# Attention and expert layer on one core: in pairs 6 and 7 of the attention, the transpose of a normalized tile is issued behind a step's two transposes of probabilities instead of ahead of them

## The chip, the core and the metric

One NeuronCore of a Trainium2 chip runs the whole program. The metric is the device time of one execution in microseconds (us); the time of a kernel is the median of several executions.

## What is computed

The reference is a layer of two parts over x of shape 2 x 2048 x 1024 in float32. Cut to what matters here:

```python
def attention(x, wq, bq, wk, bk, wv, bv, wo, bo):      # 16 heads of 64
    q, k, v = (split_heads(x @ w.T + b) for w, b in ((wq, bq), (wk, bk), (wv, bv)))
    scores = einsum('bqhd,bkhd->bhqk', q, k) / 8, causal mask
    return merge_heads(softmax(scores) @ v) @ wo.T + bo
x = x + layernorm(attention(layernorm(x)))
x = x + layernorm(expert_ffn(layernorm(x)))            # 8 experts, gate by argmax
```

Only the attention part, and of it the way from `layernorm(x)` to q, k and v for the second of the two sequences, is touched.

## The kernel before

**Numbers in two halves.** All large products run on TensorE in float16, each operand as a high and a low half (`hi`, `lo`), with three products per tile: low x high, high x low, high x high.

**Pairs and steps.** There are 16 pairs of heads (`PAIRS`): pairs 0 to 7 belong to the first sequence, pairs 8 to 15 to the second. A pair is worked off in 17 steps (`NSTEP`). A step covers up to 8 blocks of 128 keys for each of the pair's two heads, so it is two tasks, and a pair has 34 tasks. In step i of pair p the engines do the following (the `body` function of each engine):

- TensorE (L608): `scores` of the step three ahead (`LAG = 3`), then a part of a projection (`project`, L573) of the next pair's q, k or v, then `times_v` (L535) of step i itself, which multiplies the transposed probabilities `pt` by v.
- VectorE: the row maxima of the scores, and the first read of a finished projection. ScalarE: exponentials (`probs`, L914) and their high half (`hl`, L921), the high halves of the projections and of the weights. GpSimd: the low half of the probabilities (L1072).
- SyncE (SP, L429): the DMAs. For the step three ahead it issues two transposes `pt<-hl` (`transpose_probs`, L412), one per head, each of 128 x 2048 float16 numbers. It also loads the next weights (`w_raw`, L410), stores finished rows (`o_scratch`, L426), and loads and stores the tiles of the second sequence.

The order of SyncE's issues is the order in which its `body` is written. There is no scheduler. Each engine works in its own order and waits for semaphores.

**Rings.** `hl` and `pt` each hold five tasks. `transpose_probs` waits until GpSimd has finished the low half of its task (`p_lo_done`) and until `times_v` has read the ring's old content, five tasks back (`pv_done`). ScalarE in turn waits, before it writes `hl` again, until the transpose of the task five back has landed (`pt_done`, L920).

**The normalized tiles of the second sequence.** Over pairs 0 to 6 the 16 tiles of 128 rows of the second sequence are normalized beside the attention and stored in `xn_scratch` (L439). In pairs 6 and 7 they are read back with a transpose, `arena<-xn_scratch` (`transpose_x`, L401), again 128 x 2048 float16 numbers each. This comes late because the destination `xt` (in `arena`) still holds the first sequence until the projections of pair 7 have read it:

```python
TURN_CHUNKS = [0, 1, 3, 2]
TURN_TILES = [4 * c + i for c in TURN_CHUNKS for i in range(4)]
TURN_STEPS = {"pre": {i: n for n, i in enumerate((6, 7, 9, 10, 11, 13, 14, 16))},
              "turn": {i: 8 + n for n, i in enumerate((0, 1, 3, 4, 5, 7, 8, 9))}}
```

"pre" is pair 6, "turn" is pair 7. Eight of the transposes stand in steps 6, 7, 9, 10, 11, 13, 14 and 16 of pair 6, eight in steps 0, 1, 3, 4, 5, 7, 8 and 9 of pair 7. Numbered 0 to 15 in that order, numbers 0 to 3 fill chunk 0 of `xt`, 4 to 7 chunk 1, 8 to 11 chunk 3, and 12 to 15 chunk 2.

**Who needs them.** During pair 7 TensorE projects for pair 8, the first of the second sequence. By `UNITS` and `UNIT_STEPS` its units come as k and v of chunk 0 in steps 0 and 1, k of chunk 1 in step 2, v of chunk 1 and q of chunks 0 and 1 in steps 3 to 6, k of chunk 3 in step 7, v and q of chunk 3 in steps 8 to 11, k of chunk 2 in step 12, then v and q of chunk 2. Before a unit of a chunk, `project` waits for that chunk's transposes (L580 to L583):

```python
if p == HALF_PAIRS:
    tiles = LN_TILES - PE_TILES + 4 * (TURN_CHUNKS.index(c) + 1)
    for i in range(4):
        pe.wait_ge(xt_done[i], 4 * tiles)
```

So number 7 is needed in step 2 of pair 7, number 11 in step 7, and number 15 in step 12. TensorE works in order: while it waits there, `times_v` of the same step waits behind it.

Of the kernel before, what the change touches and what calls it, by code (L numbers as in the profile page):

```python
# [41 lines left out]
HALF_PAIRS = PAIRS // B  # L42
# [110 lines left out]
LN_TILES = S // P  # L153
# [6 lines left out]
def norm_tiles(p, i, part):  # L160
    return [tile for tile, at in NORM_STEPS.items() if at[part] == (p, i)]
# [4 lines left out]
# [3 lines that stand above are left out]
# [20 lines left out]
def attend_phase(nc, x, w_pairs, mask_in, xn_scratch, o_scratch, arena, fin):  # L189
    with ExitStack() as ctx:  # L190
# [48 lines left out]
        xn_stored = sem("xn_stored")  # L239
# [19 lines left out]
        unit_done = sem("unit_done")  # L259
# [66 lines left out]
        def weight_at(p, m):  # L326

            return 3 * p + ({"k": 1, "v": 2, "q": 3} if p else {"v": 1, "k": 2, "q": 3})[m]

        def next_split(p, i):  # L330

            p, i = divmod(p * NSTEP + i, NSTEP)
            kind = KIND.get(p, "mid")
            m = SPLITS[kind].get(i) if p >= 0 else None
            target = p + 1 if m == "q" or kind == "first" and i == 1 else p + 2
            return (target, m) if m and target < PAIRS else None

        def units_before(p, needed):

            return N_UNIT * p + max(u for u, unit in enumerate(order_of(p)) if unit in needed) + 1  # L340
# [14 lines left out]
        def half_done(p):  # L355

            return first_step(p, N_ROUND // 2)
# [9 lines left out]
        def pt_of(n):  # L367
            return pt[:, 2 * PT_AT[n]:2 * (PT_AT[n] + TASK_BLOCKS[n]), :]
# [24 lines left out]
        @block.sync  # L393
        def _(sp):
            def load_x(tile, sem_, b, t):
                sp.dma_start(tile, x_view[b, t]).then_inc(sem_, 16)

            def transpose_x(n, i, source):

                tok = i * P  # L400
                sp.dma_start_transpose(xt.rearrange("p l k n -> p (l k) n")[:, :, tok:tok + P], source).then_inc(  # L401
                    xt_done[n % 4], 16)

            def load_first_weight(m):
                sp.dma_start(first_raw[m], w_pairs[0, WHICH[m]]).then_inc(first_loaded[m], 16)

            def load_weight(p, m):
                if weight_at(p, m) > 1:
                    sp.wait_ge(w_lo_done, weight_at(p, m) - 1)
                sp.dma_start(w_raw[:], w_pairs[p % HALF_PAIRS, WHICH[m]]).then_inc(w_loaded, 16)  # L410

            def transpose_probs(p, i):  # L412
                for h in range(2):
                    n = NTASK * p + 2 * i + h
                    read = max([n - T_RING] + PT_BEFORE[n]) + 1
                    if read >= 1:
                        sp.wait_ge(pv_done, read)
                    sp.wait_ge(p_lo_done, n + 1)
                    sp.dma_start_transpose(pt_of(n), hl_of(n, 2)).then_inc(pt_done[n % T_RING], 16)

            def store_rows(p, half):

                sp.wait_ge(o_lo_done, 2 * p + half + 1)
                for which in range(2):
                    first = min(slot_of(rounds_of(p)[r][which]) for r in range(4 * half, 4 * half + 4))
                    sp.dma_start(o_scratch[p // HALF_PAIRS, first:first + 4, :, p % HALF_PAIRS].rearrange("t p c -> p t c"),  # L426
                                 o_hl[:, which].rearrange("p t l c -> p t (l c)")).then_inc(o_stored, 16)

            def body(p, kind):  # L429
                for i in range(NSTEP):  # L430
                    n = TURN_STEPS.get(kind, {}).get(i)
                    if n is not None:
                        tile = TURN_TILES[n]
                        sp.wait_ge(xn_stored, 16 * (tile + 1))
                        sp.wait_ge(unit_done, units_before(HALF_PAIRS - 1, [(m, tile // 4) for m in "qkv"]))
                        transpose_x(LN_TILES + n, tile, xn_scratch[tile])
                    for tile in norm_tiles(*((p, i - 1) if i else (p - 1, NSTEP - 1)), 2):
                        sp.wait_ge(xn_lo_done, LN_TILES + tile + 1)
                        sp.dma_start(xn_scratch[tile], xn[:]).then_inc(xn_stored, 16)  # L439
                        if tile + 1 < LN_TILES:  # L440
                            load_x(x_in[:], x_loaded[X_RING], 1, tile + 1)
                    if p == 0 and i == 0:
                        load_x(x_in[:], x_loaded[X_RING], 1, 0)
                    step = step_of(p, i, kind)
                    if step:
                        transpose_probs(*step)
                    split = next_split(p, i - 1)
                    if split:
                        target, m = split
                        after = {"q": (target + 1, "k"), "k": (target, "v"), "v": (target, "q")}[m]  # L450
                        if after[0] < PAIRS:
                            load_weight(*after)

                    if kind == "last" and i == NSTEP - LAG:
                        fin["load_o"](sp, 0)
                        fin["load_x"](sp, 0)
                    if i == (half_done(p) + 2 if kind != "last" else NSTEP - LAG):
                        store_rows(p, 0)
                    if p > 0 and i == 2:
                        store_rows(p - 1, 1)  # L460

                    if kind == "last":
                        for k in ([0, 1] if i == 0 else [i + 1] if i < KT - 2 else []):
                            if k == 0:
                                sp.wait_ge(s_done, NTASK * (PAIRS - 1))
                            if k == 4:
                                sp.wait_ge(pv_done, NTASK * (PAIRS - 1))
                            if k == 6:
                                sp.wait_ge(w_lo_done, 3 * PAIRS)
                            sp.dma_start(wo_raw[k], fin["w_view"][k]).then_inc(wo_loaded[k], 16)  # L470
                    if kind == "last" and i == KT - 1:
                        sp.wait_ge(unit_done, N_UNIT * PAIRS)
                        sp.wait_ge(mix_set, 2)
                        for tile, source in fin["row_loads"]:
                            sp.dma_start(tile, source).then_inc(rows_loaded, 16)
                    if kind == "last" and i == KT:

                        sp.wait_ge(wo_lo_done, 1)
                        sp.dma_start(wo_raw[KT - 1], fin["w_view"][KT - 1]).then_inc(wo_loaded[KT - 1], 16)
                    if kind == "last" and KT <= i < KT + 3:  # L480
                        for tile, source in fin["loads"][2 * (i - KT):2 * (i - KT + 1)]:
                            sp.dma_start(tile, source).then_inc(fin_loaded, 16)
                    if kind == "last" and i == NSTEP - LAG:
                        fin["load_o"](sp, 1)
                        fin["load_x"](sp, 1)
                if kind == "last":
                    store_rows(p, 1)

            load_x(x_first[0], x_loaded[0], 0, 0)
            load_first_weight("v")  # L490
            sp.dma_start(fin["ident"][:], fin["ident_in"]).then_inc(consts_loaded, 16)
            sp.dma_start(mask[:], mask_in).then_inc(consts_loaded, 16)
            for i in range(1, X_RING):
                load_x(x_first[i], x_loaded[i], 0, i)
                if i in (3, 5):
                    load_first_weight({3: "k", 5: "q"}[i])
            for i in range(LN_TILES):
                sp.wait_ge(xn_lo_done, i + 1)
                if i + X_RING < LN_TILES:
                    load_x(x_first[i % X_RING], x_loaded[i % X_RING], 0, i + X_RING)  # L500
                if i >= PE_TILES:
                    transpose_x(i, i, first_hl(i))
            load_weight(1, "k")
            for i in range(LAG):
                if i == 2:
                    load_weight(1, "v")
                transpose_probs(0, i)
            pairs(body)
# [1319 lines left out]
```

## Time and profile before

| | us |
|---|---|
| median of 3 executions (2395.73 to 2400.45) | 2397.23 |
| the profiled execution | 2399.07 |
| its span, first to last instruction | 2396.9 |
| TensorE busy (95% of the span) | 2274.4 |
| ScalarE busy (73%) | 1746.3 |
| VectorE busy (71%) | 1690.6 |
| GpSimd busy (69%) | 1654.6 |

The profile comes from one execution. Busy times are sums over the span and mix stages with different limits. In it PE is TensorE's matmuls, PEld its weight loads, DVE VectorE, ACT ScalarE, POOL GpSimd, and SP SyncE, whose instructions only issue DMAs; the time of an SP instruction is the time that the issue took, not the transfer's. "To landing" is the time from the issue's start until the transfer's semaphore is complete. PEclk is TensorE's granted clock as a share of the full 2.4 GHz. The DMA share is what the packets took, as a share of the core's 16 DMA engines, and can be above 1. Pairs 6 and 7 lie between about 790 and 1049 us of the span.

### The profile page before, as it was taken

To read this page: it belongs to the slowest core of one execution; us is meant where nothing else is said; L and a number is where in the kernel's file an instruction comes from. 1 tells how busy PE (TensorE), PEld (TensorE's weight loads), DVE (VectorE), ACT (ScalarE), POOL (GpSimd) and SP (SyncE) were. 2 spreads that over 40 slices of the span, in tenths; PEclk is the share of its full clock that TensorE was granted. 3 is DMA by queue.
4 is the path that set the end of the run, shared out by engine and by line. 5 is a ranking of instruction groups with operands and counts; after the bars stand their busy time and mean duration, and the time that the engine had idled before them with its cause. 6 is when DMAs were issued, how large, how long until landed. Compare 5 with 4: busy or idle time off the path is not lost. (4 is left out here: it accounts for less than half of the span.)

```text
span 2396.9 us, 70748 instructions
## 1 busy us (share of the span) xinstructions
PE 2274.4 (95%) x28698; PEld 1449.8 (60%) x28698; DVE 1690.6 (71%) x4148; ACT 1746.3 (73%) x2380; POOL 1654.6 (69%) x1291
## 2 busy tenths in 40 slices
PE   7999999999999998899999999999999679999996
PEld 4566667675757665557575757575766445445453
DVE  7587777777777765566666666666776846777777
ACT  5577777877787776677777777777787846666665
POOL 3588888888888876778888888888898822222221
PEclk9999999999999999999999999999999879999998
DMA  6699999999999999999999999999999976666662
GB/s 205 129 190 204 197 213 204 203 203 208 209 202 196 211 198 194 199 200 193 179 194 178 191 183 185 181 186 185 185 195 202 224 165 153 168 153 172 149 168 80
DMA packets 1372307, 445.33 MB, mean 186 GB/s; under 512 B 1316784, under 2 KB 1349952, under 8 KB 1371984
## 3 DMA queue, kind: packets, MB, share of 16 engines
q1 hardware_dynamic: 1371984, 440.81, 98.8%
q8 instruction: 228, 3.74, 0.6%
q14 instruction: 95, 0.78, 0.1%
HBM read 67.95 MB, written 41.94 MB: 46 GB/s over the span
## 5 line engine op out<-in xcount | busy, mean ns | idle before, releaser
L1072 POOL TENSOR_TENSOR hl<-probs,hl 128x1024 f16<-128x1024 f32 x544 | 1169.2, 2156 | 161.2 <-ACT hl L921 160.4
L914 ACT ACTIVATE probs<-s_ps,exp_bias 128x1024 f32<-128x1024 f32 (+7 forms) x768 | 633.7, 854 | 289.7 <-DVE exp_bias L742 289.4
L737 DVE TENSOR_REDUCE neg_max<-s_ps 128x1 f32<-128x1024 f32 (+7 forms) x768 | 676.5, 905 | 152.9 <-PE s_ps L529 149.9
L921 ACT ACTIVATE hl<-probs 128x1024 f16<-128x1024 f32 x544 | 575.0, 1057 | 85.8 <-DMA pt<-hl 69.8
L552 PE MATMUL o_ps<-v,pt 128*128 128x65 f16 x4352 | 432.5, 193 | 46.3 <-DMA pt<-hl 42.5
L552 PEld LDWEIGHTS o_ps<-v,pt 128*128 128x128 f16 x4352 | 401.4, 97 | 74.8 <-DMA pt<-hl 30.4
L553 PE MATMUL o_ps<-v,pt 128*128 128x65 f16 x4352 | 432.9, 194 | 0.0
L529 PE MATMUL s_ps<-nat 64*128 64x512 f16 (+3 forms) x3840 | 410.1, 351 | 23.5 <-ACT probs L914 20.7
L554 PE MATMUL o_ps<-v,pt 128*128 128x65 f16 x4352 | 431.6, 193 | 0.0
L553 PEld LDWEIGHTS o_ps<-v,pt 128*128 128x128 f16 x4352 | 400.6, 97 | 19.2
L554 PEld LDWEIGHTS o_ps<-v,pt 128*128 128x128 f16 x4352 | 401.2, 98 | 0.0
L602 PE MATMUL u_ps<-arena,w 128*128 128x512 f16 x1000 | 381.0, 381 | 6.0 <-DMA arena<-xn_scratch 3.1
L603 PE MATMUL u_ps<-arena,w 128*128 128x512 f16 x1000 | 379.2, 379 | 0.0
L604 PE MATMUL u_ps<-arena,w 128*128 128x512 f16 x1000 | 379.2, 379 | 0.0
L598 PE MATMUL u_ps<-w,arena 128*128 128x128 f16 x2016 | 347.6, 221 | 5.3 <-issue 3.9
L599 PE MATMUL u_ps<-w,arena 128*128 128x128 f16 x2016 | 346.5, 220 | 0.0
L600 PE MATMUL u_ps<-w,arena 128*128 128x128 f16 x2016 | 346.3, 220 | 0.0
L529 PEld LDWEIGHTS s_ps<-nat 64*128 64x128 f16 x3840 | 162.5, 95 | 162.0 <-issue 33.1
L598 PEld LDWEIGHTS u_ps<-w,arena 128*128 128x128 f16 x2016 | 198.4, 98 | 47.5 <-issue 45.2
L599 PEld LDWEIGHTS u_ps<-w,arena 128*128 128x128 f16 x2016 | 198.7, 99 | 0.0
L600 PEld LDWEIGHTS u_ps<-w,arena 128*128 128x128 f16 x2016 | 198.7, 99 | 0.0
L602 PEld LDWEIGHTS u_ps<-arena,w 128*128 128x128 f16 x1000 | 97.5, 98 | 167.0 <-issue 66.6
(190 smaller groups left out, 3612.4 us busy)
## 6 DMA issues: line engine op xcount, KB each, us to landing
w_raw<-in_w_pairs SPq DMA_DIRECT2D x46, 576.0 KB, 5.1
o_scratch<-o_hl SPq DMA_DIRECT2D x64, 256.0 KB, 3.1
out<-result SPq DMA_DIRECT2D x31, 512.0 KB, 3.2
x_in<-in_x SPq DMA_DIRECT2D x27, 512.0 KB, 4.8
pt<-hl SPq DMA_TRANSPOSE x544, 5.4
xn_scratch<-xn SPq DMA_DIRECT2D x16, 512.0 KB, 3.7
xn<-in_x SPq DMA_DIRECT2D x11, 512.0 KB, 4.0
x_in_c<-in_x SPq DMA_DIRECT2D x10, 512.0 KB, 4.2
```

The costliest lines, as they stand in the source:

```text
L529: mm = nc.tensor.matmul(s_ps[(n + h) % S_RING][:, at:end], qk[HEADS[h], q, rows], qk[HEADS[h], k, keys], start=(q == q_lo), stop=(q == q_h ...
L552: nc.tensor.matmul(dst, lo, v_hi, start=first, stop=False)
L553: nc.tensor.matmul(dst, hi, v_lo, start=False, stop=False)
L554: mm = nc.tensor.matmul(dst, hi, v_hi, start=False, stop=last)
L598: nc.tensor.matmul(dst, xt[:, 1, k, toks], hi[:, k, :], start=first, stop=False)
L599: nc.tensor.matmul(dst, xt[:, 0, k, toks], lo[:, k, :], start=False, stop=False)
L600: mm = nc.tensor.matmul(dst, xt[:, 0, k, toks], hi[:, k, :], start=False, stop=last)
L602: nc.tensor.matmul(bank, lo[:, k, :], xt[:, 0, k, toks], start=first, stop=False)
L737: nc.vector.tensor_reduce(neg_max[:, step.round, acc, h:h + 1], s_ps[(n + h) % S_RING][:, first:end], AX_X, ALU.max, negate=True).then_inc ...
L914: last = nc.scalar.activation(probs_of(n)[:, cols], s_ps[n % S_RING][:, cols], ACT.Exp, bias=exp_bias[:, step.round, acc, h:h + 1], scale= ...
L921: nc.scalar.activation(hl_of(n, 0), probs_of(n), ACT.Copy).then_inc(p_hi_done, 1)
L1072: nc.gpsimd.tensor_tensor(hl_of(n, 1), probs_of(n), hl_of(n, 0), ALU.subtract).then_inc(p_lo_done, 1)
```

## The change

In SyncE's `body` the block that issues `transpose_x` moves from the head of the step to behind `transpose_probs`, and with that also behind the store of a normalized tile and the load of the next one, where a step has them. It stays ahead of the weight load and of the store of rows. Its steps, its waits and its tiles stay the same.

```diff
             def body(p, kind):
                 for i in range(NSTEP):
-                    n = TURN_STEPS.get(kind, {}).get(i)
-                    if n is not None:
-                        tile = TURN_TILES[n]
-                        sp.wait_ge(xn_stored, 16 * (tile + 1))
-                        sp.wait_ge(unit_done, units_before(HALF_PAIRS - 1, [(m, tile // 4) for m in "qkv"]))
-                        transpose_x(LN_TILES + n, tile, xn_scratch[tile])
                     for tile in norm_tiles(*((p, i - 1) if i else (p - 1, NSTEP - 1)), 2):
...
                     step = step_of(p, i, kind)
                     if step:
                         transpose_probs(*step)
+                    n = TURN_STEPS.get(kind, {}).get(i)
+                    if n is not None:
+                        tile = TURN_TILES[n]
+                        sp.wait_ge(xn_stored, 16 * (tile + 1))
+                        sp.wait_ge(unit_done, units_before(HALF_PAIRS - 1, [(m, tile // 4) for m in "qkv"]))
+                        transpose_x(LN_TILES + n, tile, xn_scratch[tile])
                     split = next_split(p, i - 1)
```

The first place is SyncE in steps 3 to 5 of pair 7. `pt<-hl` is a transpose of probabilities (x4 is two steps' worth), `arena<-xn_scratch` a transpose of a normalized tile, here numbers 10, 11 and 12. Before:

```order
L401 DMA_TRANSPOSE arena<-xn_scratch 128x16x128
L419 DMA_TRANSPOSE pt<-hl 128x16x128 x2
L410 DMA w_raw<-in_w_pairs 128x1152
L401 DMA_TRANSPOSE arena<-xn_scratch 128x16x128
L419 DMA_TRANSPOSE pt<-hl 128x16x128 x2
L401 DMA_TRANSPOSE arena<-xn_scratch 128x16x128
L419 DMA_TRANSPOSE pt<-hl 128x16x128 x4
```

The same place after the change:

```order
L419 DMA_TRANSPOSE pt<-hl 128x16x128 x2
L401 DMA_TRANSPOSE arena<-xn_scratch 128x16x128
L410 DMA w_raw<-in_w_pairs 128x1152
L419 DMA_TRANSPOSE pt<-hl 128x16x128 x2
L401 DMA_TRANSPOSE arena<-xn_scratch 128x16x128
L419 DMA_TRANSPOSE pt<-hl 128x16x128 x2
L401 DMA_TRANSPOSE arena<-xn_scratch 128x16x128
```

Each tile transpose has changed places with the two probability transposes of its own step. Number 11, which step 7 needs, now stands third in its step. The weight load still follows the same set of transposes.

The second place is SyncE in steps 7 to 13 of pair 7, with numbers 13, 14 and 15, the last ones. Before:

```order
L401 DMA_TRANSPOSE arena<-xn_scratch 128x16x128
L419 DMA_TRANSPOSE pt<-hl 128x16x128 x2
L401 DMA_TRANSPOSE arena<-xn_scratch 128x16x128
L419 DMA_TRANSPOSE pt<-hl 128x16x128 x2
L401 DMA_TRANSPOSE arena<-xn_scratch 128x16x128
L419 DMA_TRANSPOSE pt<-hl 128x16x128 x6
L426 DMA o_scratch<-o_hl 128x4x256 x2
```

The same place after the change:

```order
L419 DMA_TRANSPOSE pt<-hl 128x16x128 x2
L401 DMA_TRANSPOSE arena<-xn_scratch 128x16x128
L419 DMA_TRANSPOSE pt<-hl 128x16x128 x2
L401 DMA_TRANSPOSE arena<-xn_scratch 128x16x128
L419 DMA_TRANSPOSE pt<-hl 128x16x128 x2
L401 DMA_TRANSPOSE arena<-xn_scratch 128x16x128
L419 DMA_TRANSPOSE pt<-hl 128x16x128 x4
L426 DMA o_scratch<-o_hl 128x4x256 x2
```

Number 15 has moved behind the two probability transposes issued in step 9 (those of step 12). From there on the queue is the same as before. The other engines' orders are not changed.

## Rows read from the trace of the kernel before

**Rows 1.** Stretch, length, busy us (x instructions) of PE, PEld, DVE, ACT, POOL; PEclk, DMA share, GB/s:

```profile
840.00:1060.00 220.00, 194.68 (x2703) 127.01 (x2700) 132.41 (x330) 144.88 (x195) 153.56 (x94) 0.97 1.14 196
1100.00:1220.00 120.00, 120.00 (x1717) 79.23 (x1714) 81.31 (x208) 94.00 (x123) 100.84 (x61) 1.00 1.09 186
```

**Rows 2.** Waits of PE, 840 to 1060: total us, times, longest us:

```profile
PE o_ps L552 <- DMA pt<-hl: 12.1, 10, 3.1
PE s_ps L529 <- ACT probs L914: 6.8, 4, 3.4
PE u_ps L602 <- DMA arena<-xn_scratch: 3.1, 1, 3.1
PE o_ps L552 <- issue: 3.0, 2, 2.5
```

**Rows 3.** Timeline of SP, 835 to 1030: start us, length us, what, count:

```profile
847.42 2.50 SPq L401 DMA_TRANSPOSE arena<-xn_scratch  x1
...
972.30 3.46 SPq L401 DMA_TRANSPOSE arena<-xn_scratch  x1
...
1012.98 2.40 SPq L401 DMA_TRANSPOSE arena<-xn_scratch  x1
1015.47 16.61 SPq L419 DMA_TRANSPOSE pt<-hl  x6
```

**Rows 4.** Transposes issued from 847 to 1019, by line: duration ns min/median/max:

```profile
L419 SPq DMA_TRANSPOSE pt<-hl x43: 1497/2849/4263, 845.5 to 1018.3; - x43
...
L401 SPq DMA_TRANSPOSE arena<-xn_scratch x16: 1583/2463/5419, 847.4 to 1013.0; - x16
```

**Rows 5.** Timeline of POOL, 1000 to 1008, low half for the issue at 1018.3:

```profile
1005.15 2.12 POOL L1072 TENSOR_TENSOR hl<-probs,hl 128x1024 f16<-128x1024 f32 x1
```

**Rows 6.** The `pt<-hl` issues at 979.8 and at 1018.3, each with its landing:

```profile
L419 SPq DMA_TRANSPOSE pt<-hl x1: 2806/2806/2806, 979.8 to 979.8; - x1
...
DMA to landing us min/median/max: 4.3/4.3/4.3
...
L419 SPq DMA_TRANSPOSE pt<-hl x1: 1497/1497/1497, 1018.3 to 1018.3; - x1
...
DMA to landing us min/median/max: 5.3/5.3/5.3
```

**Rows 7.** Timeline of PE in short windows, 939 to 1059:

```profile
939.48 0.39 PE L602 MATMUL u_ps<-arena,w 128*128 128x512 f16 x1
...
980.43 0.38 PE L602 MATMUL u_ps<-arena,w 128*128 128x512 f16 x1 [3.06 <-DMA arena<-xn_scratch]
...
1008.64 0.20 PE L552 MATMUL o_ps<-v,pt 128*128 128x65 f16 x1 [3.12 <-DMA pt<-hl]
...
1018.07 0.39 PE L602 MATMUL u_ps<-arena,w 128*128 128x512 f16 x1
...
1030.37 0.20 PE L552 MATMUL o_ps<-v,pt 128*128 128x65 f16 x1 [0.58 <-DMA pt<-hl]
...
1048.23 0.20 PE L552 MATMUL o_ps<-v,pt 128*128 128x65 f16 x1 [0.50 <-DMA pt<-hl]
...
1058.79 0.39 PE L529 MATMUL s_ps<-nat 64*128 64x512 f16 x2 [1.51 <-ACT probs L914]
```

**Rows 8.** Timeline of ACT, 1051 to 1058:

```profile
1056.43 1.06 ACT L894 ACTIVATE w<-w_raw 128x1024 f16<-128x1024 f32 x1 [3.27 <-DMA w_raw<-in_w_pairs]
```

**Rows 9.** Stretches of 4 us with a lowered clock (columns as in rows 1):

```profile
888.00:892.00 4.00, 1.28 (x32) 1.19 (x33) 0.30 (x2) 2.57 (x4) 1.46 (x1) 0.79 0.84 173
892.00:896.00 4.00, 4.00 (x36) 1.98 (x33) 0.18 (x1) 2.74 (x6) 4.00 (x4) 0.50 1.16 227
896.00:900.00 4.00, 4.00 (x79) 4.00 (x78) 3.93 (x6) 3.78 (x4) 2.34 (x2) 0.86 1.09 239
...
1008.00:1012.00 4.00, 3.36 (x43) 1.96 (x44) 0.86 (x4) 2.58 (x3) 2.19 (x2) 0.72 1.13 235
1012.00:1016.00 4.00, 4.00 (x41) 2.10 (x42) 3.98 (x13) 2.70 (x4) 3.14 (x2) 0.85 0.99 190
```

## The prediction, made before the changed kernel was run

> **What bounds the kernel now.** I read the views in this order.
>
> First the busy time by stretch. Between 1100 and 1220 us, in pair 8, TensorE is busy for all 120.00 us. Between 840 and 1060, where the tile transposes lie, it is busy for 194.68 of 220 us, so about 25 us are idle [rows 1]. The rest of the attention is bound by TensorE, and this stretch is not.
>
> Then TensorE's waits there [rows 2]. 12.1 us are waits for a probability transpose to land (`DMA pt<-hl`), and 3.0 us more stand before the same line L552. 6.8 us are waits for ScalarE's exponentials. 3.1 us, in one piece, are a wait for a tile transpose.
>
> Then SyncE's timeline [rows 3]. The reader is to see that it has no holes: the issue that starts at 1012.98 takes 2.40 us, and the next starts at 1015.47, six in a row take 16.61 us, 2.77 each. An issue takes as long as the transfers ahead of it need. From 847 to 1019 there are 43 probability transposes with a median of 2.85 us and 16 tile transposes with a median of 2.46 [rows 4]. The 16 add 16 x 2.46 = 39 us to a queue that has little room, and part of that comes out as the 25 us.
>
> Last, whether the queue waits for its inputs. The low half whose transpose is issued at 1018.3 was finished at 1005.15 + 2.12 = 1007.27 [rows 5, 6]. It had been ready for 11 us. So **the queue of transposes bounds this stretch**, and it works through its list without a pause.
>
> **What the change does to the queue.** It removes and adds no instruction. Every step issues the same DMAs, and while the queue has a backlog only the order within a step counts. In each of 16 steps the two probability transposes move up past one tile transpose and land about 2.5 us earlier (one issue, [rows 4]). The tile transpose moves back past two of the others, about 5.7 us. In the one step of pair 6 with both, it also passes the store of a tile, whose content TensorE needs much later. Weight loads and stores of rows keep their place, since the same transposes stand ahead of them. SyncE's waits for the projections that free `xt` were met long before. Cost on the queue: nothing, as long as the backlog of 11 us lasts. If it did not last, an engine that is late would be handed on to the queue; that is a rival below.
>
> **What the earlier probabilities give.** TensorE idles less where it waits for probabilities of a step with a tile transpose. But a wait removed in the middle is only moved: TensorE next meets a transpose that has not moved. The waits at 1030.37 and at 1048.23 are for steps 13 and 16 of pair 7, behind the last tile transpose, where before and after the queue has done the same work [rows 7]. Up to there the gain is counted as 0.
>
> **What the later tile transposes cost.** Three of them have a near deadline.
>
> Number 7 moves to about 939 or 940 (the old end of its step in the queue), and its projection starts at 939.48 [rows 7]. That costs under 1 us, and TensorE soon waits for other things. Counted as 0.
>
> Number 11, issued at 972.30 [rows 3], is waited for already: TensorE idles 3.06 us until 980.43 [rows 7]. Now it takes the third place of its step, which is the landing of the issue at 979.8, 979.8 + 4.3 = 984.1 [rows 6]. The wait ends 3.7 us later. TensorE has several us of waits for unmoved probabilities behind it before 1031, so this is paid back. Counted as 0.
>
> Number 15, issued at 1012.98, is free now. TensorE starts k of chunk 2 at 1018.07 without a wait [rows 7]. In the changed order the third place of that step lands at 1018.3 + 5.3 = 1023.6 [rows 6]. So **TensorE stands until 1023.6, which is 5.5 us later**, whatever came before it.
>
> What of the 5.5 us is paid back: the waits of 0.58 us at 1030.37 and of 0.50 us at 1048.23, since those transposes land at their old times. Also the 1.51 us at 1058.79 [rows 7]. There ScalarE had waited 3.27 us for a weight load [rows 8], which is issued by the queue at its old time, so that a late ScalarE finds it there. After that nothing is left: the list of TensorE's waits between 1060 and 1700 is empty. 5.5 - 0.6 - 0.5 - 1.5 = 2.9 us remain.
>
> **The clock.** After idle pieces of some 3 us the granted clock has fallen to its lower level, 1.2 GHz: behind the 3.12 us that end at 1008.64 [rows 7] the slices show 0.72 and 0.85, a loss of (0.28 + 0.15) x 4 = 1.7 us of full-rate time. Behind the two close waits around 890 they show 0.79, 0.50 and 0.86, a loss of 3.4 us [rows 9]. Behind the 3.06 us at 980 it did not fall. A wait of over 5 us, with a full projection right behind it, is more than any of these. No row has one so long, so the bounds are 0 and 3.4 us. I take 1.7, the loss behind the longest single wait nearby. The Trainium skill, in "TensorE: Matmul & The Clock Gate", section "Why this matters for your kernels", advises against idle gaps between bursts of matmuls because the clock drops behind them. That speaks against this change. By that rule the 1.7 us is due; by the row at 980 alone it would be 0 and the sum 2.9.
>
> **The sum.** 2.9 + 1.7 = 4.6 us later. The profiled execution takes 2399.07 us, so this one would take 2403.7. It lies 1.84 us above the median of 2397.23, within the spread of the three runs (2395.73 to 2400.45), so I carry the difference over to the median: 2397.23 + 4.6 = **2401.8 us**, 0.19% slower. About 0.2%, 4.8 us, is what a measurement of this kernel can tell from no change, and the forecast lies just inside.
>
> A second estimate of the delay can be had from a rate. The Trainium skill, in "DMA: Bandwidth & Descriptors", section "Latency and other measured facts", gives 261 GB/s for a DMA transpose. A transpose of 512 KB would then take 2.0 us, number 15 would be delayed by 4.0 us behind two of them, and the sum would be about 2.9 us. The rows say 2.85 us for one, so the trace does not agree, and I stay with the rows.
>
> **The rivals.**
>
> *A longer stretch at the low clock (slower).* The place is step 12 of pair 7. If TensorE needs twice as long to get its clock back, as around 890, the loss is 3.4 us and the sum 2.9 + 3.4 = 6.3 us: 2403.5. It decides when TensorE meets a second short gap within the first microseconds of its work. For it: the wait is longer than any before. Against it: a whole projection of about 5 us follows without a gap. In the same direction, with less chance: TensorE's lateness in steps 7 to 13 delays scores and low halves by 5 to 7 us. Should that use up the backlog, the queue runs dry and the 3.7 us of number 11 are not paid back: 4.6 + 3.7 = 8.3 us, 2405.5. Against it: the backlog was 11 us at 1018.
>
> *The wait without the clock.* The sum is 2.9 us, 2400.1. For it: the clock stayed up behind the 3.06 us at 980.
>
> *The wait does not bind (no change).* If number 15 still lands before about 1020.7, because the three transposes of a step overlap more in the new order, or TensorE is late by itself in step 12, the remainder is paid back and the time stays at 2397.2. Against it: step 12 starts at 1018.07, and the third place has to gain 3 us.
>
> *Probabilities first pays (faster).* If the stretch is bound by the probabilities' latency and not by the queue's length, the waits in steps with a tile transpose go for good. That would be up to 15.1 us of [rows 2] less those in steps that have not moved, of which I can name 0.6 and 0.5 us, and I take half, 7 us: 2390. It decides if the queue is found without a backlog. Against it stand the 11 us that a ready task lies [rows 5, 6].
>
> **How the numbers follow.** Forecast 0.40, longer clock loss 0.27, queue runs dry 0.04, wait without clock 0.12, wait does not bind 0.12, probabilities first 0.05. Slower by over 0.2% is both slower rivals, 0.31, and 0.15 of the forecast's 0.40, which lies at the border: 0.46. Within 0.2% is the other 0.25 with 0.12 and 0.12: 0.49. Faster 0.05. The range has to take in no change (2397.2 less 0.7 for the scatter of a median) and the clock's upper bound with 1 us each for the landing and the scatter and half of the dry queue: 2396.5 to 2406.0.
>
> **What would show it.** In the changed profile the waits of PE on `arena<-xn_scratch` should be about three, some 0.5, 7 and 5.5 to 6.5 us long, ending near 940, 984 and 1023.6, in place of the one of 3.1 us. Waits of PE on `pt<-hl` should shrink to a few us in all, and the one at 1008.64 should be gone or small. SyncE's timeline should still have no holes up to 1040. The waits at 1030, 1048 and 1058 should be gone, and the clock should show a low stretch from about 1023. The forecast is wrong if number 15 lands with TensorE still busy before it, if the last transposes of pair 7 land several us earlier or later than before, or if the difference between the kernels arises outside 840 to 1060.

## The result, and the profile after

The changed kernel takes 2403.43 us (median of 20 executions, 2397.68 to 2411.06), the kernel before 2397.84 us (median of 20, 2394.96 to 2403.93). The ratio is 1.0024, with a 95% interval of 1.0017 to 1.0030: **slower by 0.24%, 5.6 us**. The forecast was 4.6 us, in a range of 2396.5 to 2406.0. The second set of runs of the same two kernels, on another occasion, gives 1.0024 (1.0012 to 1.0035).

The profiled execution of the changed kernel took 2404.84 us, with a span of 2402.6 us. TensorE's waits between 840 and 1060 us, columns as in [rows 2]:

```profile
PE u_ps L602 <- DMA arena<-xn_scratch: 13.7, 3, 8.9
PE s_ps L529 <- ACT probs L914: 7.0, 2, 6.3
PE o_ps L552 <- DMA pt<-hl: 6.5, 4, 2.7
PE u_ps L602 <- DVE full L711: 0.6, 1, 0.6
```

The waits for probabilities have fallen from 12.1 us, with 3.0 more marked "issue", to 6.5 [rows 2]. The waits for tile transposes have risen from 3.1 us to 13.7, in three pieces. Here are their ends on TensorE's timeline, and two rows behind them:

```profile
938.66 0.38 PE L602 MATMUL u_ps<-arena,w 128*128 128x512 f16 x1 [0.50 <-DMA arena<-xn_scratch]
...
983.34 0.59 PE L602 MATMUL u_ps<-arena,w 128*128 128x512 f16 x1 [8.95 <-DMA arena<-xn_scratch]
...
1020.52 0.58 PE L602 MATMUL u_ps<-arena,w 128*128 128x512 f16 x1 [4.22 <-DMA arena<-xn_scratch]
...
1043.13 0.38 PE L602 MATMUL u_ps<-arena,w 128*128 128x512 f16 x1 [0.57 <-DVE full L711]
```

The three are for numbers 7, 11 and 15, as the prediction had said. The fourth is a wait for VectorE that every profile of this case has. It serves as a mark for the end of the stretch. The matmuls at 983 and 1020 last 0.59 and 0.58 us instead of 0.38, which is the lower clock.

SyncE's timeline of the changed kernel, columns as in [rows 3]:

```profile
969.93 8.34 SPq L419 DMA_TRANSPOSE pt<-hl  x2
978.36 2.43 SPq L401 DMA_TRANSPOSE arena<-xn_scratch  x1
...
988.69 10.69 SPq L419 DMA_TRANSPOSE pt<-hl  x4
...
1010.68 4.62 SPq L419 DMA_TRANSPOSE pt<-hl  x2
1015.39 1.84 SPq L401 DMA_TRANSPOSE arena<-xn_scratch  x1
1017.33 13.17 SPq L419 DMA_TRANSPOSE pt<-hl  x4
```

The issues between 840 and 1020, columns as in [rows 4]:

```profile
L419 SPq DMA_TRANSPOSE pt<-hl x46: 1317/2627/4225, 837.3 to 1017.3; - x46
```

Number 11 is now issued at 978.36 and number 15 at 1015.39, each behind its step's two probability transposes.

The prediction expected no holes in this list up to 1040. There are some, and the list hides them: a row such as the one at 988.69 joins several issues and the pauses between them. These are single issues, from the same timeline in windows of 1 us or less:

```profile
988.69 1.92 SPq L419 DMA_TRANSPOSE pt<-hl  x1
...
991.82 1.77 SPq L419 DMA_TRANSPOSE pt<-hl  x1
...
1023.09 3.28 SPq L419 DMA_TRANSPOSE pt<-hl  x1
...
1029.17 1.32 SPq L419 DMA_TRANSPOSE pt<-hl  x1
```

SyncE stands from 990.6 to 991.8 and from 1026.4 to 1029.2. Both times it waits for TensorE: the second transpose of a step needs the place in `pt` that `times_v` frees two steps earlier, and TensorE is late because it has itself waited for number 11, or for number 15. From the weight load to the mark, both defined below, all of SyncE's pauses over 0.13 us add up to 5.0 us in this profile, to 2.0 us in a second one of the same kernel, and to 0.3 us in each of the two profiles of the kernel before.

Absolute times of two profiles can't be compared directly, since the work ahead of the stretch varies by almost 5 us between executions. I therefore measure from the weight load that SyncE issues in step 5 of pair 6, ahead of the first tile transpose in all kernels, to the mark. For the kernel before these are the rows at 834.09 and 1038.72:

```profile
834.09 0.57 SPq L410 DMA_DIRECT2D w_raw<-in_w_pairs  x1
...
1038.72 0.38 PE L602 MATMUL u_ps<-arena,w 128*128 128x512 f16 x1 [0.40 <-DVE full L711]
```

That is 204.6 us before. After the change the load is at 832.22, so it is 1043.13 - 832.22 = 210.9 us, **6.3 us more in this stretch**. Then comes what is still paid back, TensorE's waits from the start of step 12's projection up to 1700. First the kernel before:

```profile
PE s_ps L529 <- ACT probs L914: 1.5, 1, 1.5
PE o_ps L552 <- DMA pt<-hl: 1.1, 2, 0.6
PE u_ps L602 <- DVE full L711: 0.4, 1, 0.4
```

The same view of the changed kernel has one row:

```profile
PE u_ps L602 <- DVE full L711: 0.6, 1, 0.6
```

Of the 1.1 us, the 0.58 us at 1030.37 lie before the mark and are already inside the 6.3. The 0.50 us at 1048.23 and the 1.5 us lie behind it [rows 7] and are gone, so 4.3 us are left. No wait follows: TensorE is busy for all 640 us from 1060 to 1700.

```profile
1060.00:1700.00 640.00, 640.00 (x9237) 428.36 (x9234) 433.35 (x1093) 498.31 (x651) 531.30 (x317) 1.00 1.08 185
```

One pair of profiles does not give the difference to a microsecond. From the mark to the last instruction these two take 1358.2 us (before) and 1359.5 us (after), and the profiles of all kernels here that compute everything lie between 1355.8 and 1360.0 us. The medians decide.

### The profile page after: what moved, and what is told of

It reads as the page before. It is cut to its first block and busy times, and to the rows that moved or that the text cites. A ratio compares the mean times of both kernels' runs of the same rounds, so it can differ in the third digit from the quotient of the medians.

```text
span 2402.6 us, 70748 instructions
## 1 busy us (share of the span) xinstructions
PE 2277.6 (95%) x28698; PEld 1450.3 (60%) x28698; DVE 1691.4 (70%) x4148; ACT 1746.5 (73%) x2380; POOL 1654.8 (69%) x1291
## 5 line engine op out<-in xcount | busy, mean ns | idle before, releaser
L552 PE MATMUL o_ps<-v,pt 128*128 128x65 f16 x4352 | 432.0, 193 | 35.9 <-DMA pt<-hl 29.6
L552 PEld LDWEIGHTS o_ps<-v,pt 128*128 128x128 f16 x4352 | 401.5, 97 | 64.0 <-issue 22.5
L529 PE MATMUL s_ps<-nat 64*128 64x512 f16 (+3 forms) x3840 | 411.4, 352 | 26.3 <-ACT probs L914 23.5
L602 PE MATMUL u_ps<-arena,w 128*128 128x512 f16 x1000 | 382.7, 383 | 16.8 <-DMA arena<-xn_scratch 13.7
L529 PEld LDWEIGHTS s_ps<-nat 64*128 64x128 f16 x3840 | 163.3, 95 | 165.4 <-issue 38.6
L598 PEld LDWEIGHTS u_ps<-w,arena 128*128 128x128 f16 x2016 | 198.1, 98 | 47.1 <-issue 44.8
L602 PEld LDWEIGHTS u_ps<-arena,w 128*128 128x128 f16 x1000 | 97.9, 98 | 178.5 <-issue 78.2
L716 DVE TENSOR_SCALAR full<-u_ps,bias_cols 128x512 f32<-128x512 f32 x125 | 93.8, 751 | 156.1 <-PE u_ps L604 152.5
L1085 POOL TENSOR_TENSOR o_rows<-o_long,inv_long 128x128 f32<-128x128 f32 x128 | 74.4, 581 | 186.3 <-DVE inv_long L778 185.9
```

Of the source, the lines that this page charges most:

```text
L529: mm = nc.tensor.matmul(s_ps[(n + h) % S_RING][:, at:end], qk[HEADS[h], q, rows], qk[HEADS[h], k, keys], start=(q == q_lo), stop=(q == q_h ...
L552: nc.tensor.matmul(dst, lo, v_hi, start=first, stop=False)
L598: nc.tensor.matmul(dst, xt[:, 1, k, toks], hi[:, k, :], start=first, stop=False)
L602: nc.tensor.matmul(bank, lo[:, k, :], xt[:, 0, k, toks], start=first, stop=False)
```

## The experiments

Theory A is the prediction's: the queue of transposes bounds the stretch, earlier probabilities give nothing at its end, and the cost is the wait for number 15, since it comes too late to be paid back. The other theories are told with each run. Most experiments use one switch in SyncE's `body`, which puts each tile transpose ahead or behind by its number n. The line numbers of these kernels are 1 to 13 higher than those of the kernel before (where the switch alone is in, L609 is L602, L559 is L552 and L536 is L529; with the weight loads moved, L565 is L552 and L542 is L529).

The kernel before was timed again beside them, and the ratios are against these times: 2399.50 us (35 executions) for the first four experiments, 2399.25 us (21) for the next four, 2399.92 us (10) for the second profiles. The ratio and its interval differ from the quotient of the two medians by up to 0.0006; differences in us are worked out from the ratio, unless they are called differences of medians.

```diff
+BEHIND = {...}
...
-                    if n is not None:
+                    if n is not None and n not in BEHIND:
                         tile = TURN_TILES[n]
...
                         transpose_probs(*step)
+                    if n is not None and n in BEHIND:
+                        tile = TURN_TILES[n]
...
+                        transpose_x(LN_TILES + n, tile, xn_scratch[tile])
```

### Number 15 alone behind: `BEHIND = {15}`

> The kernel before, with only number 15, the last tile transpose, moved behind the two probability transposes of its step. Theory A (the last deadline): the cost of the change is TensorE's wait in step 12 of pair 7, so this kernel is 4 to 6 us slower than before, as the full change is; its profile has a wait of 3.5 to 6 us on arena<-xn_scratch ending about 1021 to 1024, and still the 3 us wait for number 11 near 980. Rival B (the middle): the cost comes from the 9 us wait for number 11, the long stretch at the low clock behind it and the pause of the queue that they cause; then this kernel takes the time of before, within 1 us. Rival C (every moved transpose costs a little): 5.6 / 16 = 0.35 us.

Measured: 2403.55 us, ratio 1.0020 (1.0011 to 1.0029), **4.8 us slower**. One moved transpose of 16 costs what the whole change costs, within the intervals. The end of its wait in step 12:

```profile
1020.75 0.59 PE L609 MATMUL u_ps<-arena,w 128*128 128x512 f16 x1 [5.16 <-DMA arena<-xn_scratch]
```

The wait for number 11 is 2.15 us in this profile. Rivals B (0) and C (0.35 us) fall: both lie outside the interval, 2.6 to 7.0 us.

### The other 15 behind, number 15 ahead: `BEHIND = set(range(15))`

> The changed kernel, with number 15 put back ahead of the probability transposes of its step. Theory A: within 1 us of before; the 9 us wait for number 11 is there in the profile and is paid back by 1049 us, step 12 starts without a wait. Rival B: 4 to 6 us slower than before, as the full change. Rival C: 15 x 0.35 = 5.2 us slower.

Measured: 2400.82 us, ratio 1.0001 (0.9992 to 1.0010), no difference clear of the noise of about 2 us. Fifteen of the 16 moves together cost nothing that can be seen. Two views of its profile show how. The wait for number 11 is there, long and followed by the low clock:

```profile
985.65 0.58 PE L609 MATMUL u_ps<-arena,w 128*128 128x512 f16 x1 [6.83 <-DMA arena<-xn_scratch]
```

And behind step 12 TensorE still waits for the queue, 1.0 us, and for ScalarE, 1.7 us, as the kernel before does. Its step 12 starts at 1018.59, 181.9 us behind the weight load (at 836.72), against 184.0 and 184.6 us in the two profiles of the kernel before. It is on time again:

```profile
PE s_ps L536 <- ACT probs L921: 1.7, 1, 1.7
PE o_ps L559 <- DMA pt<-hl: 1.0, 2, 0.8
PE u_ps L609 <- DVE full L718: 0.6, 1, 0.6
```

Rivals B and C, which had expected 4 to 6 us, fall. The pause of the queue that rival B names is there, 1.1 us behind 993.1, and costs nothing.

### Number 11 alone behind: `BEHIND = {11}`

> The kernel before, with only number 11 moved behind. Theory A: within 1 us of before; the wait for number 11 grows from 3.1 to 7 to 9 us and TensorE's later waits for probabilities (1.7, 3.1, 0.6, 0.5 us before) shrink by as much. Rival B: 4 to 6 us slower. Rival C: 0.35 us slower.

Measured: 2399.71 us, ratio 0.9999 (0.9989 to 1.0009), no difference.

```profile
983.35 0.59 PE L609 MATMUL u_ps<-arena,w 128*128 128x512 f16 x1 [7.83 <-DMA arena<-xn_scratch]
```

The wait grows from 3.1 to 7.8 us and is paid back in full: the waits of 1.7 and 3.1 us for probabilities that follow before are not there, and behind step 12 0.7 and 1.7 us of waits are left. The queue pauses for 1.5 us behind 990.4, also without a cost. Rival B falls, rival C (0.35 us) is too small for this interval.

From weight load to mark this profile takes 1036.38 - 834.29 = 202.1 us, and that of the 15 moved takes 1038.66 - 836.72 = 201.9 us, 2.5 and 2.7 us less than before, although the times are the same. So the length of the stretch in a single profile scatters by some 3 us.

### The deadlines ahead, the rest behind: `BEHIND = set(range(16)) - {7, 11, 15}`

> The changed kernel, with the three tile transposes that have a near deadline (numbers 7, 11 and 15) put back ahead, the other 13 behind. Theory A: the earlier probabilities give nothing at the end of the stretch, so within 1 us of before. Rival B: the same. Rival C: 13 x 0.35 = 4.6 us slower. Rival D (earlier probabilities do pay where no deadline is missed): 2 us or more faster than before, since TensorE's waits for probabilities in the stretch (15 us) shrink and nothing takes their place.

Measured: 2399.28 us, ratio 0.9993 (0.9983 to 1.0002). Rival C (4.6 us slower) falls. Rival D (2 us faster or more) is neither shown nor excluded: the ratio is 1.7 us faster, the medians differ by 0.2 us, the interval runs from 4 us faster to 0.5 us slower. Its profile has waits of 3.9 and 1.6 us for tile transposes: those with a deadline now stand right behind their predecessors, numbers 10 and 14, which moved back.

### Number 15 two places late

> The kernel before, with number 15 moved two places late: behind the probability transposes issued in step 10 of pair 7. Theory A: it lands one step of the queue (5.5 to 6 us) later than in the kernel with number 15 alone moved, everything that could be paid back is used up, so each further microsecond counts in full: 10 to 12 us slower than before, and one wait of 10 to 11 us in step 12. Rival E (the queue gives a late TensorE its time back, because it has more room behind the last tile transpose): the loss stays near 5 us.

```diff
-              "turn": {i: 8 + n for n, i in enumerate((0, 1, 3, 4, 5, 7, 8, 9))}}
+              "turn": {i: 8 + n for n, i in enumerate((0, 1, 3, 4, 5, 7, 8, 10))}}
+BEHIND = {15}
```

Measured: 2408.40 us (4 runs), ratio 1.0035 (1.0021 to 1.0048), 8.4 us slower. The wait ends later and is longer:

```profile
1025.81 0.59 PE L609 MATMUL u_ps<-arena,w 128*128 128x512 f16 x1 [8.57 <-DMA arena<-xn_scratch]
```

Measured from the weight load at 834.11 that is 191.7 us, 5.4 and 3.8 us later than in the two profiles with one place (186.3 and 187.9), and from weight load to mark it takes 1047.76 - 834.11 = 213.7 us, 9.0 more than before, against 3.0 and 6.0 in the two profiles with one place. The time is below the 10 to 12 us expected, since the wait is 8.6 us and not 10 to 11; the interval of 4 runs, 5.0 to 11.5 us, doesn't exclude either. Nor does it exclude rival E (it stays near 5 us). The profile speaks against E, as no wait is left behind step 12 from which the delay could be paid back, and so for the view that the further delay counts. It is one profile, with the scatter of 3 us named above.

### The tile transposes left out

> The kernel before without the 16 tile transposes of pairs 6 and 7 and without TensorE's wait for them; q, k and v of the second sequence are computed from stale data. Theory A (the queue's sum bounds the stretch): TensorE's idle time of about 25 us between 840 and 1060 goes, and with it the low clock, so 22 to 30 us faster. Rival F (latency and not the sum: only single waits behind a tile transpose, the rest of the idle time comes from ScalarE's and VectorE's extra work there): under 12 us faster.

```diff
-                        transpose_x(LN_TILES + n, tile, xn_scratch[tile])
...
-                    if p == HALF_PAIRS:
-                        tiles = LN_TILES - PE_TILES + 4 * (TURN_CHUNKS.index(c) + 1)
-                        for i in range(4):
-                            pe.wait_ge(xt_done[i], 4 * tiles)
```

Measured: 2371.63 us (4 runs), ratio 0.9880 (0.9867 to 0.9894), **28.8 us faster**. TensorE in the stretch, columns as in [rows 1]:

```profile
840.00:1060.00 220.00, 218.10 (x3038) 141.06 (x3036) 155.92 (x381) 171.72 (x226) 179.79 (x112) 1.00 1.11 189
```

218.1 of 220 us are busy and the clock is 1.00 throughout, against 194.7 and 0.97 before. No wait for probabilities is listed there. Rival F (under 12 us) falls. From weight load to mark it takes 1012.12 - 837.01 = 175.1 us, 29.5 less than before, and behind the mark the same as before (1357.9 and 1358.2 us), so the gain arises in the stretch. SyncE's pauses there add up to 12.8 us, against 0.3 before. All but 2 us of TensorE's idle time goes with the 16 transposes, 28.8 / 16 = 1.8 us of the time for each, while the waits for a tile transpose itself made up only 3.1 us before. This fits the prediction's basis, that the sum of the queue's work bounds the stretch. The run takes out work and waits together, so the other orders, which keep the sum and the time, have to bear the rest of that argument.

### The weight loads ahead

> The kernel before, with the weight load of a step in pairs 6 and 7 issued ahead of the step's probability transposes instead of behind them. Theory A: ScalarE no longer waits for the load, so TensorE's waits for exponentials near 928, 952 and 1058 us shrink; only the last one (1.5 us) is not followed by a wait for the queue, so 0 to 2 us faster. Rival G (those waits are an independent cost): 5 to 6 us faster. Rival H (a weight load ahead delays the probabilities at 1048 by its own 3 us): 1 to 3 us slower.

```diff
+                    split = next_split(p, i - 1)
+                    if split and kind in ("pre", "turn"):
...
+                            load_weight(*after)
                     step = step_of(p, i, kind)
...
-                    if split:
+                    if split and kind not in ("pre", "turn"):
```

Measured: 2398.32 us, ratio 1.0001 (0.9992 to 1.0010), no difference. TensorE's waits, 840 to 1062:

```profile
PE o_ps L565 <- DMA pt<-hl: 18.4, 13, 3.4
PE o_ps L565 <- issue: 1.9, 2, 1.0
PE s_ps L542 <- ACT probs L927: 1.5, 4, 0.7
```

The waits for exponentials go from 6.8 to 1.5 us, and those for probabilities from 12.1 to 18.4. All of TensorE's waits add up to 25.0 us, against 25.4 before: the idle time has changed its name only. Rivals G (5 to 6 us faster) and H at its upper half (over 2.4 us slower) fall.

### Both together

> Numbers 7, 11 and 15 ahead, the other 13 tile transposes behind, and the weight loads of pairs 6 and 7 ahead of the probability transposes. Theory A: the sum of the queue's work is the same, so 0 to 3 us faster than before. Rival G: 6 us or more faster.

The edits are those of the two runs before. Measured: 2398.42 us, ratio 0.9992 (0.9984 to 1.0001). It has the lowest ratio of all versions that compute everything, but it can't be told from the kernel before. TensorE's waits between 840 and 1062 add up to 20.2 us in its profile, less than the 25.4 before, so their sum alone doesn't give the time either. Rival G (6 us or more) falls.

### Second profiles

> The changed kernel once more, for a second profile: how far the sizes of the terms vary. Theory A: again three waits for tile transposes, the last one 3.5 to 6 us long and followed by a stretch at the low clock, none of TensorE's later waits up to 1700 us except the 0.6 us for VectorE, and 3 to 7 us slower than before. If the last wait is near 4 us again, the queue works the last step off faster than was predicted; if the low clock lasts 3.4 us this time, its length is chance.

Measured: 2406.20 us, ratio 1.0024 (1.0012 to 1.0035).

```profile
1025.10 0.59 PE L602 MATMUL u_ps<-arena,w 128*128 128x512 f16 x1 [5.88 <-DMA arena<-xn_scratch]
...
1046.45 0.38 PE L602 MATMUL u_ps<-arena,w 128*128 128x512 f16 x1 [0.58 <-DVE full L711]
```

With the weight load at 835.78 the stretch takes 210.7 us (210.9 in the first profile). The last wait is 5.9 us long this time and ends 189.3 us behind the load, in the first profile 188.3. In the kernel before the same matmul starts 1018.07 - 834.09 = 184.0 us behind it. So number 15 costs 4.3 and 5.3 us against that profile. In the second profile of the kernel before (next) it starts at 1021.21, 184.6 us behind the load, and against that the cost is 3.7 and 4.7 us.

> The kernel before once more, for a second profile. Theory A: step 12 of pair 7 starts without a wait for number 15, the total of TensorE's idle time between 830 and 1060 is 23 to 26 us again, ending with waits for probabilities behind the last tile transpose and one for ScalarE behind the weight load.

One time, 2400.42 us. From the load at 836.59 to the mark at 1041.27 it takes 204.7 us (204.6 in the first profile). Step 12 has no wait for number 15. The idle time in the list of waits is 22.7 us, just under the 23 to 26 expected. The waits for probabilities that were expected behind the last tile transpose are not there, and the one for ScalarE is 0.5 us.

> Number 15 alone behind, a second profile. Theory A: a wait of 4 to 6 us in step 12 of pair 7 and, behind it, no wait for probabilities or for ScalarE up to 1700 us.

One time, 2405.30 us. The wait in step 12 is 5.4 us, and nothing but the mark's own 0.6 us follows:

```profile
PE u_ps L609 <- DVE full L718: 0.6, 1, 0.6
```

From load to mark it takes 1046.13 - 835.53 = 210.6 us, against 207.6 in the first profile. The two profiles of this kernel differ by 3 us, the two of before and the two of the change by 0.2 at most. Much of the 3 us had arisen before number 15: up to number 11 this kernel's order is that of the kernel before, and its wait for number 11 ends 143.8 and 145.2 us behind the load, against 146.3 and 146.4 before.

## Why the prediction was right

**What bounds the stretch: right, though what was read for it was not enough.** The queue's sum does. Without the tile transposes the stretch is TensorE's again, and 28.8 us go. The kernels with tile transposes and weight loads in another order change where TensorE is idle and what it waits for, and not the time, as long as number 15 keeps its place.

The prediction showed it by a list of issues without holes and by one low half that had been ready for 11 us. The list alone shows nothing. In pair 8, where TensorE is busy for 120 of 120 us [rows 1], it looks the same, and a pause of 1.9 us is hidden in this row:

```profile
1109.37 31.22 SPq L419 DMA_TRANSPOSE pt<-hl  x10
```

And a probability transpose has a second input, the place in `pt` that `times_v` frees five tasks back. SyncE's own list of waits, 847 to 1030, even names TensorE:

```profile
SPq L419 <- PE o_ps L554: 41.4, 26, 4.3
```

But that list takes any end of `times_v` that falls into an issue, and not the one that is needed. By the ring, the issue at 1018.3 (step 12, second head) needs `times_v` of step 10, first head, which had ended when TensorE's wait of 3.12 us before 1008.64 began, at 1005.5 [rows 7]. It had been free for almost 13 us. Worked out like this for every issue from 840 to 1062 of the kernel before, both inputs were ready 2.5 us or more ahead; in pair 8 one of them is often ready less than 1 us ahead. So the queue did bound the stretch.

**Earlier probabilities counted as 0: right, within the noise.** TensorE waits less for them (6.5 us after, 15.1 before). All but number 15 moved: 1.0001, with an interval of 2 us to either side, so a gain or a cost below that isn't excluded.

**Number 11 counted as 0: right, with a wait longer than said.** It waits 8.95 and 8.8 us instead of 7. Behind the weight load the wait ends at 151.1 and 151.4 us, 4.8 to 5.1 later than before (146.3 and 146.4) and not 3.7, and TensorE comes to it 0.6 to 1.1 us earlier. It is paid back: `only_11` is at 0.9999. The prediction's reason, waits for "unmoved probabilities" behind it, holds for one of the two large ones only. The wait that ends at 1008.64 is for step 10, whose transposes are issued in step 7 together with number 13, and so move. **Number 7**, "under 1 us", waits 0.50 us in the first profile and not at all in the second.

**Number 15, 5.5 us: the mechanism right, the size on the large side.** The term was read as the old landing of the third place of the step, 1023.6, when nothing ahead had changed, which is 189.5 us behind the weight load. Measured are 188.3 and 189.3 us, and a cost of 3.7 to 5.3 us, by which profile of the kernel before is taken. In the first profile the queue had come to the step a little sooner: the issue at 1015.39 is 183.2 us behind the weight load, while the last probability transpose of that step had been issued at 1018.3, 184.2 us behind it.

The Trainium skill's 261 GB/s ("DMA: Bandwidth & Descriptors", "Latency and other measured facts") would have given an estimate of 3.8 us for this term: two transposes of 2.0 us, less the 0.2 us or so by which number 15 had landed before TensorE came. The rows gave 5.5, and what was measured lies between the two or just below. For one transpose the trace does not agree with that figure: the probability transposes' median issue was 2.63 us in the changed kernel and 2.85 before [rows 4], against 2.0.

**What is paid back, 0.6, 0.5 and 1.5 us: right for the first profile of the kernel before.** All three waits are gone in both profiles of the change. But the second profile of the kernel before has only 0.5 us of them to begin with, so the term is 0.5 to 2.6.

**The clock, 1.7 us: between the two sizes measured.** The slices behind the last wait of the changed kernel:

```profile
1020.00:1024.00 4.00, 3.48 (x9) 1.28 (x10) 0.00 (x0) 2.39 (x3) 3.51 (x3) 0.50 1.08 209
1024.00:1028.00 4.00, 4.00 (x16) 1.60 (x15) 0.00 (x0) 0.17 (x1) 2.12 (x1) 0.78 1.23 154
```

From 1020.52 to 1024 at half rate, 1.7 us, and 0.22 x 4 = 0.9 us in the next slice: 2.6 us lost. In the second profile the clock is lower from about 1024.3 to 1027.8 only, with work from 1025.10 on, 1.3 us lost. The slices of that profile:

```profile
1024.00:1028.00 4.00, 2.90 (x8) 1.11 (x9) 0.00 (x0) 0.88 (x1) 2.67 (x2) 0.57 1.35 181
1028.00:1032.00 4.00, 4.00 (x33) 2.00 (x32) 0.23 (x1) 1.06 (x1) 2.03 (x1) 1.00 1.08 229
```

The "longer stretch" that the prediction gave its slower rival came in one of two profiles, but worth 0.9 us more than the forecast and not 1.7. By the rule of the Trainium skill ("TensorE: Matmul & The Clock Gate", "Why this matters for your kernels") a loss was due behind such a gap, and the trace agrees.

**The sum.** With the measured terms and the first profile of the kernel before: 4.3 + 2.6 - 2.6 = 4.3 and 5.3 + 1.3 - 2.6 = 4.0 us. Against its second profile: 3.7 + 2.6 - 0.5 = 5.8 and 4.7 + 1.3 - 0.5 = 5.5 us. Each agrees within 0.1 us with what the lengths from load to mark and the waits behind it give (4.3, 4.0, 5.7 and 5.5 us), and the 5.6 us of the medians (interval 4.1 to 7.2) lie among them. So no further term is needed. That the forecast came within 1 us is in part luck: its delay was on the large side, its clock loss lay between two values that differ by a factor of two, and what is paid back changes by 2 us from one profile of the kernel before to the other.

**The rivals.** "The wait does not bind" and "probabilities first pays" (7 us faster) are out: the first by `only_15`, the second by `all_but_15`.

"The queue runs dry" did happen for short times, against the expectation, and did not decide. The prediction read the backlog at 1018, behind the wait for number 11, and found 11 us. At the issue at 992.80 of the kernel before, which has to follow `times_v` of step 7, it was only 6.3 us, and TensorE's wait for number 11 grew by 5.9 us. So the queue paused there (1.1 us and 0.1 us in the two profiles), as it did in `only_11` and `all_but_15`, which lost nothing. Behind number 15 it paused for 2.7 and 1.5 us, and the weight load of step 14, at 1051.71 in the kernel before, was issued 219.0 and 218.4 us behind the first one, against 217.6 and 216.1 before, and not "at its old time". TensorE was so late by then that it found every transpose. ScalarE still waited for that weight load, 0.7 and 1.1 us against 3.3 before, but TensorE did not wait for ScalarE. With number 15 two places late the pause is 8.0 us, and the DMA engines move 4 GB/s between 1028 and 1032, again without a wait of TensorE's behind it:

```profile
1028.00:1032.00 4.00, 4.00 (x16) 1.63 (x15) 0.00 (x0) 0.00 (x0) 0.00 (x0) 0.79 0.02 4
```

**Where the text was weak.** It put the chance of slower by over 0.2% at 0.46, and the result is just beyond that border. The forecast of 4.6 us stood 0.2 us on the other side. And the upper end of its range, 2406.0, does not follow from the parts that it names, which add up to 2403.5 + 1 + 1 + 1.9 = 2407.4; the result lies inside either.

## What to carry to other kernels

Where a queue with a backlog bounds a stretch, its sum sets the end, and the order in it decides mostly which consumer waits; look for the item with a deadline that has no queue-bound wait behind it, because a delay there is the only one that is kept. Judge a wait by what follows it: the 9 us for number 11 cost nothing, the 4 to 6 us for number 15 cost nearly all they are. A wait that disappears from the profile is not a gain until the end of the stretch has moved. And read a backlog from each input of the queue at the place where the consumer will be late; a merged timeline without holes doesn't show one.

## What was not expected of the hardware

A gap of 2.15 us was followed by the lower clock. In the profile of `only_15` TensorE stands until 978.34, and the slices behind show 0.88 and 0.69, 1.7 us of full-rate time.

```profile
976.00:980.00 4.00, 1.85 (x8) 0.72 (x7) 3.65 (x12) 0.25 (x1) 0.37 (x1) 0.88 1.20 179
980.00:984.00 4.00, 4.00 (x14) 1.59 (x13) 0.00 (x0) 2.81 (x4) 2.12 (x1) 0.69 0.94 178
```

Five profiles have this wait for number 11 with the same order ahead of it. The clock fell behind gaps of 2.15, 2.95, 3.05 and 3.15 us, and stayed up behind the 3.06 us of the first profile of the kernel before. So the length of the gap alone does not decide there, and a forecast needs both cases.

And the time of the whole kernel scatters by some 9 us between executions (2394.96 to 2403.93 before). The two profiles of the bound stretch of the kernel before agree within 0.1 us (204.6 and 204.7), but that is not its scatter: `only_15` shows 207.6 and 210.6, and `only_11` and `all_but_15`, which take the time of the kernel before, 202.1 and 201.9.
